# Eight-block transformer on one Trainium2 core: the two routed-expert blocks run on from the attention before them, their routing spread through the loops

## The reference

```
x = x + attention over the 16 heads of each row (width 8), output by Wfc   # stage 5
x = x + experts(layernorm(x))                                              # stage 6
x = x + full attention of batches of 512 rows, 2 heads of 64, with norms   # stage 7
x = x + experts(layernorm(x))                                              # stage 8

experts(x):  logits = x @ Ws.T + bs              # 8 experts
    probs  = softmax(logits); routes = argmax(probs); x = x * max(probs)
    perm   = argsort(routes, stable=True)        # rows sorted by expert
    h = relu(x @ W1[e] + b1[e]);  y = h @ W2[e] + b2[e]
    output: y of each row's expert, in sorted order
```

## Time and profile before

| | us |
|---|---|
| median of 3 runs (lowest, highest) | 1938.3 (1935.96, 1942.25) |
| the profiled execution | 1945.4 |
| its span, first to last instruction | 1943.6 |
| PE, PEld, DVE, ACT, POOL busy | 1622.5, 1160.9, 1223.0, 1069.2, 906.4 |
| granted TensorE clock, mean | 0.911 |

### The profile page before, as it was taken

One profiled execution on the slowest core, in us unless ns is written; L12 is line 12 of the kernel. 1 busy time (PEld: TensorE's weight loads), 2 busy tenths in 40 slices (PEclk: granted clock), 3 DMA queues, 4 the chain that ended last, 5 costly groups with the idle time before them and its releaser, 6 DMA issues.

```text
span 1943.6 us, 37984 instructions
## 1 busy us (share of the span) xinstructions
PE 1622.5 (83%) x13323; PEld 1160.9 (60%) x13323; DVE 1223.0 (63%) x3746; ACT 1069.2 (55%) x2751; POOL 906.4 (47%) x668
## 2 busy tenths in 40 slices
PE   5999997799999966889887789999976666958787
PEld 5999995566666633334544466666644544646565
DVE  3556554887777634555763788777736975636555
ACT  3655563788888724556542578888842113324332
POOL 1333333776666511323443777667613673422134
PEclk8999998999999986999876899999987987968979
DMA  5000000111111100000000111111100001210012
GB/s 206 1 1 1 1 2 6 26 33 31 28 26 29 26 3 1 1 1 1 2 1 1 24 27 32 26 33 26 32 7 0 1 1 38 23 27 1 22 23 23
DMA packets 41082, 38.64 MB, mean 20 GB/s; under 512 B 21944, under 2 KB 32192, under 8 KB 40512
## 3 DMA queue, kind: packets, MB, share of 16 engines
q1 hardware_dynamic: 35264, 32.02, 6.3%
q0 software_dynamic: 5632, 4.20, 1.8%
HBM read 13.14 MB, written 4.20 MB: 9 GB/s over the span
## 4 chain that ended last, share of the span: by engine, by line
PE 46%; DVE 15%; issue 12%; POOL 7%; ACT 4%; POOLq 0%; DMA 0%; DVEq 0%; ACTq 0%; SPq 0%; another core or an unknown queue 0%
PE ps L682 4%; PE ps L328 3%; PE ps L483 3%; PE ps L586 3%; PE ps L492 3%; PE ps L900 3%; PE ps L529 3%; PE ps L908 2%; PE ps L495 2%; PE ps L543 2%; PE ps L598 2%; PE ps L695 2%; PE ps L561 2%; PE ps L502 2%; DVE g_ss L1639 2%
## 5 line engine op out<-in xcount | busy, mean ns | idle before, releaser
L977 ACT ACTIVATE arena<-ps 128x512 f32<-128x512 f32 (+4 forms) x670 | 356.6, 588 | 284.2 <-PE ps L328 103.8
L1214 ACT ACTIVATE arena<-ps 128x320 f32<-128x320 f32 (+4 forms) x256 | 132.4, 561 | 137.4 <-PE ps L682 134.5
L1114 ACT ACTIVATE arena<-arena,g_small 128x128 f32<-128x128 f32 x512 | 198.7, 406 | 0.5
L2197 POOL TENSOR_TENSOR arena<-arena,consts 128x512 f32<-128x512 f32 (+1 forms) x64 | 93.2, 1456 | 196.1 <-ACT arena L1214 196.0
L1610 DVE CUSTOM_DVE_ANT_0 arena<-ps,consts,g_ss 128x128 f32<-128x128 f32 x512 | 145.6, 347 | 58.7 <-PE ps L483 58.7
L2218 POOL TENSOR_TENSOR arena<-arena 128x512 f32<-128x512 f32 x64 | 81.8, 1278 | 176.8 <-DVE arena L1618 176.8
L682 PE MATMUL ps<-arena 32*128 32x160 f32 (+4 forms) x1024 | 122.3, 468 | 20.9 <-ACT arena L1214 10.2
L328 PE MATMUL ps<-consts,arena 128*128 128x128 f32 x400 | 80.9, 340 | 68.7 <-POOL arena L2176 19.5
L1617 DVE TENSOR_TENSOR arena<-ps,tabs 128x512 f32<-128x512 f32 x128 | 87.7, 685 | 52.4 <-ACT arena L1083 44.9
L328 PEld LDWEIGHTS ps<-consts,arena 128*128 128x128 f32 x400 | 55.7, 172 | 106.1 <-POOL arena L2176 24.2
L682 PEld LDWEIGHTS ps<-arena 32*128 32x128 f32 x1024 | 61.9, 213 | 88.6 <-ACT arena L1214 54.2
(11 more groups left out here) (256 smaller groups left out, 4200.0 us busy)
## 6 DMA issues: line engine op xcount, KB each, us to landing
arena<-arena SPq DMA_DIRECT2D x112, 128.0 KB, 2.3
weights<-in_w SPq DMA_DIRECT2D x1, 5069.0 KB, 24.2
weights<-in_w SPq DMA_DIRECT2D x1, 2052.0 KB, 12.7
arena<-Y SPq DMA_DIRECT2D x64, 32.0 KB
arena<-Y SPq DMA_DIRECT2D x64, 31.8 KB
consts<-in_c SPq DMA_DIRECT2D x1, 1278.0 KB, 8.7
sorted_rows<-X SPq DMA_DIRECT2D x1, 1024.0 KB, 5.1
X<-sorted_rows SPq DMA_DIRECT2D x4, 256.0 KB, 3.6
```

The costliest lines, as they stand in the source:

```text
L977: copy = lambda o, i: act.activation(o, i, ACT.Copy)
L1114: last = act.activation(g_p[:, n % 2, 4 * hf + i, :], g_sc[:, 4 * hf + i, :], ACT.Exp, scale=-1.0, bias=g_mn[:, h:h + 1], accum_out=g_rs[: ...
L1214: act.activation(b_p[:, U % 2, 2 * gp:2 * gp + 2, at:at + n], ps[:, b:b + 2, 0:n], ACT.Exp, scale=float(HD) ** -0.5).then_inc(s.b_exp, 1)
L2197: pool.tensor_tensor(v, v, m.unsqueeze(1).broadcast_to([P, NG, n]), ALU.mult)\
```

## The change

1. The experts' part of the arena moves behind that of both attentions (`taken[0] = 12800`), with its own `e_stats`, `e_mv` and `e_bias`. Their PSUM banks are chosen per stage.
2. No barrier between attention and experts: each engine goes from its attention loop straight into `experts(k)`. SP writes `X` to memory as soon as its last row is added.
3. Batch 0 is routed inside the attention's last steps. On DVE in stage 5: variance of batch 0 at t = 8, centre at 9, shift at 12 (ahead of values), route at 13, prefix at 15; batch 1's variance and centre at 12 and 13, batch 2's variance after the loop. In stage 7: variances at 5, 9, 13 and after the loop, centres at 6, 10, 14, shift at 13, route at 14, prefix after the loop. PE's four steps stand at t = 10, 11, 13, 14 and at 9, 12, 14, 15.
4. Batches 1, 2, 3 are routed inside the main loop from units 0, 7, 14 on (`turned_at`). `places_of_all` follows unit 19.
5. The tail of head attention (shift(15), values(14), sums(15), values(15), the last rows) is written out after its loop, its last parts inside units 3 to 7.
6. Unit 0 no longer waits for the biases: it writes `e_acc` (mask times product, no addition); POOL adds batch 0's biases, fetched into `e_bias`, once after unit 7.

The core of the diff: banks and units; PE (stage 5 loop, a front step, main loop); ACT main loop; DVE (stage 5 loop, its tail, unit 0, main loop); POOL. Stage 7 and the functions moved out unchanged are left out.

```diff
-        taken[0] = 0
+        taken[0] = 12800
...
+        front_bank, up_banks, down_banks = (4, 7), ((0, 1), (5, 6)), ((2, 3), (0, 1))
+        turned_at = (None, 0, 7, 14)
...
+                    if t == 10:
+                        turn_routed_x(0, 0)
+                    if t == 11:
+                        logits(0, 0)
+                    if t == 13:
+                        turn_scaled_x(0, 0)
+                    if t == 14:
+                        ranks(0, 0)
+                experts(0, turn_sums, rows_out)
...
+            def turn_routed_x(k, c):
+                z = NB * k + c
+                pe.wait_ge(es.e_ln, z + 1)
+                need(pe, es.e_rank_in, z)
+                if c == 0:
+                    pe.wait_ge(s.m_xT if k else s.c_xT, NB)
...
+                    if k == 0 and q == 6:
+                        turn_sums(NB - 1)
+                    if k == 0 and q == 7:
+                        rows_out(NB - 1)
+                    for c in range(1, NB):
+                        if q == turned_at[c]:
+                            turn_routed_x(k, c)
+                        elif q == turned_at[c] + 1:
+                            logits(k, c)
+                        elif q == turned_at[c] + 5:
+                            turn_scaled_x(k, c)
+                        elif q == turned_at[c] + 6:
+                            ranks(k, c)
...
+                    if k == 0 and q == 4:
+                        norm_routed(0, 2)
+                    if k == 0 and q == 6:
+                        keep_sums(NB - 1)
+                    if q == (11 if k == 0 else 4):
+                        norm_routed(k, 3)
+                    for c in range(1, NB):
+                        if q == turned_at[c]:
+                            keep_routed_x(k, c)
+                        elif q == turned_at[c] + 2:
+                            exps_routed(k, c)
+                        elif q == turned_at[c] + 5:
+                            keep_scaled_x(k, c)
...
                     if 0 <= t - 1 < TT:
                         shift(t - 1)
+                    if t == 12:
+                        shift_routed(0, 0)
                     if 0 <= t - 2 < TT:
                         values(t - 2)
                     if 0 <= t - 1 < TT:
                         sums(t - 1)
+                    if t == 13:
+                        route(0, 0)
+                    if t == 15:
...
+                    if t in (7, 11, 15):
+                        add_rows((t - 7) // NT)
+                    if t in (8, 12):
+                        variance(0, t // NT - 2)
+                    if t in (9, 13):
+                        centre(0, t // NT - 2)
+                shift(TT - 1)
+                values(TT - 2)
+                sums(TT - 1)
+                variance(0, 2)
+                experts(0, values, add_rows)
...
+                        if q == 0:
+                            ins = ts(e_acc[:, i, :], ps[:, down_banks[k][0], j * P:(j + 1) * P], e_oh[:, i, 0:1], None,
+                                     ALU.mult)
+                            continue
...
+                    if k == 0 and q == 3:
+                        values(TT - 1)
+                        centre(0, 2)
+                    if k == 0 and q == 7:
+                        add_rows(NB - 1)
+                        variance(0, 3)
+                    if q == (9 if k == 0 else 1):
+                        centre(k, 3)
+                    for c in range(1, NB):
+                        if q == turned_at[c]:
+                            shift_routed(k, c)
+                        elif q == turned_at[c] + 1:
+                            route(k, c)
+                        elif q == turned_at[c] + 5:
+                            prefix(k, c)
+                    if q == turned_at[3] + 5:
+                        places_of_all(k)
...
+                fetch_biases(0)
+                fetch_biases(1)
+                if k == 0:
+                    root_routed(0, 3)
+                fetch_biases(2)
+                pool.wait_ge(b2_sem[0], 16 * NT * (k + 1))
+                pool.wait_ge(es.e_acc_in, (E * NB - 1) * k + E)
+                pool.tensor_tensor(e_acc[:, 0:NT, :], e_acc[:, 0:NT, :], e_bias, ALU.add).then_inc(es.e_bias_in, 1)
+                fetch_biases(3)
```

More of the change, by code:

```diff
@@ new lines, in full_attention, with norm_routed @@
+                    if t in (7, 11, 15):
+                        norm_routed(1, t // NT - 1)
+                    if t == 9:
+                        keep_routed_x(1, 0)
+                    if t == 13:
+                        exps_routed(1, 0)
+                    if t == 14:
+                        keep_scaled_x(1, 0)
+                experts(1)
+            def norm_routed(k, c):
+                act.wait_ge(es.e_nm, NB * k + c + 1)
+                for i in range(NT * c, NT * c + NT):
+                    last = act.activation(e_xl[:, i, :], X[:, i, :], ACT.Identity,
+                                          scale=e_rstd[:, i:i + 1], bias=e_nm[:, i:i + 1])
+                last.then_inc(es.e_ln, 1)
@@ new lines, in full_attention, with by_expert, variance @@
+                    if t in (5, 9, 13):
+                        variance(1, t // NT - 1)
+                    if t in (6, 10, 14):
+                        centre(1, t // NT - 1)
+                    if t == 14:
+                        route(1, 0)
+                dve.wait_ge(s.m_out, TT)
+                variance(1, 3)
+                prefix(1, 0)
+                experts(1)
+            def by_expert(ap):
+                return ap.unsqueeze(2).broadcast_to([P, NT, E])
+            def variance(k, c):
+                for i in range(NT * c, NT * c + NT):
+                    last = dve.bn_stats(e_stats[:, i, :], X[:, i, :])
+                after(last)
+                for i in range(NT * c, NT * c + NT):
+                    last = dve.bn_aggr(e_mv[:, i, :], e_stats[:, i, :])
+                after(last)
+                ts(e_rstd[:, NT * c:NT * c + NT], e_mv[:, NT * c:NT * c + NT, 1], EPS5, None, ALU.add)\
+                    .then_inc(es.e_var, 1)
@@ new lines, in places_of_all @@
+            def places_of_all(k):
+                dve.wait_ge(es.e_rank_in, NB * k + NB)
+                for e in range(E - 1):
+                    after(tt(e_eo[:, e + 1:e + 2], e_eo[:, e:e + 1], e_pre[:, TT, e:e + 1], ALU.add))
+                after(tt(e_pos, e_pos, wide(e_eo, [P, TT, E], 1), ALU.add))
+                after(tt(e_pos, e_pos, e_oh, ALU.mult))
+                after(dve.tensor_reduce(e_m[:, 5], e_pos, AX, ALU.add))
+                dve.tensor_copy(e_idx[:, :], e_m[:, 5]).then_inc(es.e_idx_in, 1)
```

401 lines of the change are left out of this document (159 added, 242 removed).

## The result

The changed kernel takes 1931.8 us (median of 7 runs, 1928.1 to 1937.8) where the kernel before took 1940.1 beside it: a ratio of 0.9963, 95% interval 0.9948 to 0.9978, or 7.2 us less. In nine later runs it gave 1931.9 and the same 0.9963. The direction was forecast, the size was not: 19.3 us were predicted, and 1919 with 1907 to 1931.

What follows compares the result with a forecast made beforehand. POOL's sends, starting when the places end, were taken to bound both expert stages' ends. Gains of 7.7 us in stage 6 and 11.6 in stage 8 made 19.3, so 1938.3 - 19.3 = 1919 us, range 1907 to 1931.

Steps and rivals of the forecast that it cites:

- Port waits: Head attention: DVE's small operations wait for POOL's mixes, 2.9 us at t = 8, 9, 12, 4.9 at 13; none beside fetches.
- PE's lower clock in head attention: Stage 5, t = 14: PE's sum takes longer after idleness, 1.2 us taken from between 0 and 2.8.
- Unit 0 to the places in stage 6: Stage 6: DVE's own work of 41.4 us plus waits of 10.3, from 1618.6 to places ending at 1670.3.
- The exit: Stages 6 and 8: sixteen POOL sends in a row at 1.86 us end 29.8 us after the places.
- rival of a slow memory: Exits of both stages: sends at 3.1 us each would cost 37 more, giving 1956; chance 0.05.
- Full attention: Stage 7: batch 0's routing adds 7.9 us, 3.8 of it in step 14; then 2.2 for turning, up(1) and down(0).
- The end: After stage 8's last send: no added time was predicted.
- 7.7: Stage 6: us gained, its sends ending at 1700.1 against 1707.8.
- 11.6: Stage 8: us gained, its sends ending at 1928.7 against 1940.3.
- the scale: Whole kernel: the profile's 1945.4 lies 7.1 us above the median, so 19.3 was subtracted from 1938.3.
- gain is eaten: Rival: route's locked operations meet more mixes, or waits double, leaving the time within 0.3%, 1932.5 to 1944; chance 0.13.
- a late e_probs stops PE in stage 7: Stage 7, part of the rival of chance 0.13: a late e_ln or e_probs stops PE for all; no separate size.

Runs made afterwards that it cites:

- e_dve_early: Changed kernel with batch 0's variance, centre and route in head attention put behind the products, ahead of the maxima: ratio 0.9955 to the kernel before.
- e_exps_first: Changed kernel with ACT's exponentials put ahead of its copy of the turned sums at t = 6, 10, 14: 1918.5 us, ratio 0.9887 to the kernel before.
- e_before_exps: The kernel before with its exponentials of steps 6, 10 and 14 put ahead of the copy of the turned sums: ratio 0.9963.
- e_spacing8: Changed kernel with batches 1 to 3 routed eight units apart, not seven, places behind unit 21: ratio 0.9976 to the kernel before.
- e_six_apart: Changed kernel with batches 1 to 3 routed six units apart, places behind unit 17, batch 2 in a second PSUM bank: ratio 0.9928 to the kernel before.
- e_fill: Changed kernel with unread matmuls where PE waits in head attention, full attention's step 14 and stage 8's opening: ratio 0.9946 to the kernel before.
- e_all_five8: Changed kernel with exponentials first, early statistics and route, scores(15) ahead of turning, routing six units apart, in stage 8 five: 1903.1 us, ratio 0.9813.

## Why the prediction was wrong

**Port waits.** Right. Steps 8, 9, 12 and 13 of head attention grew by 2.9, 2.8, 2.9 and 4.6 us; 2.9, 2.9, 2.9 and 4.9 were forecast. Nothing of the kind shows beside POOL's fetches: route beside them takes 0.2 an operation. That the operations aren't long for themselves e_dve_early and the other places show: the centre took 2.92 us beside a mix and 0.15 in stage 7. What a barrier is worth by itself no run shows.

**PE's lower clock in head attention: this step failed.** The prediction gave it 1.2 us, at t = 14 alone, and took the place where it would strike from PE's idleness. Step 14 grew by 1.2 to 1.7, but step 10 by 3.0 in two of the six executions that share this code with the change, by 1.7 in one and by 0.1 in three, and it had been forecast at nothing: 1.9 us more in the mean of the four profiles that give the 231.0. Unit 0 came 146.7 to 150.8 us after the first products; 146.4 was forecast. The trace of before had the coupling on show, 8.0 for step 10 where steps 8 and 9 took 6.1, and I didn't ask why: the exponentials stand behind a copy that stands behind PE's sum. I had treated head attention as a chain of DVE and POOL to which PE is a bystander. e_exps_first shows it: with that order mended step 10 lasts 6.1 and step 14 6.1, with all the port waits still there. Against e_before_exps the change then brings 7.5 us in stages 5 and 6, or 9.6 from products(8) on.

**Unit 0 to the places in stage 6.** 50.6 and 52.3 us, 51.7 forecast; the wait ahead of unit 5 is 2.47, 3.2 forecast, and all the waits together are 9.6 in the first profile, 10.3 forecast. Right. **The exit:** sixteen sends at 1.87 in both stages, the last ended 30.0 and 29.8 behind the places; unit 31 done 4 us before send 12. Right, and e_spacing8 and e_six_apart move the end as the places move. The rival of a slow memory is out.

**Full attention: two terms too small, again by the lower clock.** The statistics, centres and logits cost 0.9, 0.1 and 0.8 a step as forecast. Step 14 costs 5.2, forecast 3.8: turning and scores took 3.2 us in place of 1.7. Unforecast are 1.0 to 1.6 in step 7 or 11: the second profile's step 11 lasts 7.5, before 5.95, and its values took 3.34 us where before's took 2.02, in windows of granted clock 0.79 and 1.00 (first line the changed kernel's second profile, second line the kernel before):

```profile
1806.00:1814.00 8.00, 7.72 (x47) 6.83 (x48) 4.17 (x10) 4.12 (x10) 0.00 (x0) 0.79 0.00 1
```

```profile
1807.00:1815.00 8.00, 5.34 (x43) 4.48 (x42) 4.74 (x9) 2.94 (x7) 1.83 (x1) 1.00 0.00 0
```

From maxima(5) to maxima(15) the stage grew by 9.9 and 10.4 us, where 7.9 was forecast. And unit 0 waits 4.2 and 3.8, forecast 2.2, since up and down ran at the lower clock. These surpluses don't add up to what lacks, because one thing went the other way, and that was luck: values(15) had run at the lower clock in before, and did not in the changed kernel (first line before, second line changed):

```profile
1836.99 3.63 PE L842 MATMUL ps<-arena 128*128 128x128 f32 x16 [0.83 <-ACT arena L977]
```

```profile
1835.51 2.02 PE L862 MATMUL ps<-arena 128*128 128x128 f32 x16 [0.46 <-ACT arena L1002]
```

So unit 0 came 143.9 and 144.3 us after the reload, 2.3 and 2.7 later than the 141.6 forecast; from there to the places it took 45.7 and 46.1, forecast 44.8. Over the four profiles behind the 219.4 the two excesses are 1.6 and 1.6 us, and the remaining 1.1 of the 4.3 that lack is the profile of before that I subtracted from. That the lower clock costs step 14 and the wait of unit 0 some 2.7 us is shown by e_fill; for steps 7 and 11 and the loop it is read from the clock alone.

**The end: a term put at nothing.** 2.2 us come on behind the last send in every kernel that has the change, and none in the kernels without it. It is not the data: the last send's landed 3.3 us after its start in the second profile of either kernel (in the changed one a send took 4.7, but that was the fifth of the sixteen), and SP had seen all of it 1.7 to 1.8 us after the last send's end, with the change and without. What ends later is POOL's DRAIN at the end of the program, 3.1 us behind the last send in before and 5.3 in the changed kernel (its length in ns, three times the same, then its start; the last sends end at 1940.30 and 1920.75; first line before, second line changed):

```profile
L116 POOLq DRAIN  x1: 9631/9631/9631, 1933.7 to 1933.7; - x1
```

```profile
L116 POOLq DRAIN  x1: 16319/16319/16319, 1909.7 to 1909.7; - x1
```

A broken row of sends doesn't bring it back, nor do engines that finished as late as before: in e_all_five8 unit 31 ended 6.6 us ahead of the last send's end, as in before, and the 5.5 stayed. Why POOL's DRAIN takes 2.2 us longer stays open.

**The sum.** 7.7 lost 3.5: 2.1 from products(8) on, nearly all of it step 10, and the rest in steps 0 to 7, which the change doesn't touch. 11.6 lost 4.3: about 1.6 up to unit 0, 1.6 from there to the places, 1.1 by the scale. 2.2 went at the end: 9.3 remain by the profiles, 7.2 by the timed runs, and the 2 between are less than either can tell. The scale was off because I subtracted from a median of three runs a sum that was made on one slow execution, whose stretches were 0.4 and 1.1 us over the mean of its kernel. The rival "gain is eaten" had the nearest region (1932.5 and up, the time is 0.7 below it) and mostly the wrong mechanism: no mix was caught between pieces of route. Its remark that a late e_probs stops PE in stage 7 came nearer: PE waited 3.19 us there.

## What to carry over

A wait that is put into a loop is priced with everything that queues behind it on the other engines, and the places to look at are the steps of the old trace that are already longer than their neighbours. Ask of each queue what stands ahead of the operation on the path for no reason of data: moving one call behind another took 13.4 us off the changed kernel and about 7 off the kernel before, where the whole change brought 7.2. Where PE waited more, its work took 1.6 to 1.9 times as long afterwards, so an overlap that adds waits elsewhere is worth less than the time that it covers; and profile the kernel before more than once before a sum of 20 us, 1% of the time, is made on it. When such a sum has been measured, compare it term by term: here one term came out right with 2 us of luck in it, and two that were wrong partly cancelled.

## What the runs showed of the hardware

- The same sum after the same 2.91 us of idleness took 6.65 us in one execution and 3.72 in another, at granted clocks of 0.66 and 1.00.
- The kernel before took 1932 to 1946 us in 15 executions on one chip, at mean granted clocks of 0.919 and 0.908 for the two ends.
- Two matmuls of 512 columns that nobody reads, put into PE's wait, kept the next groups at the upper clock: 0.66 and 1.13 us in place of 1.11 and 2.08.
- A DVE operation of 4 to 32 elements beside a mix of POOL took 1.1 to 2.9 us with one SBUF input or two; beside POOL's indirect fetches, 0.2. The Trainium skill (SBUF — State Buffer, Who interferes with whom) lets a GpSimd operation that reads SBUF shut out a DVE operation with two SBUF inputs. It also names `tensor_scalar` among the operations that can take the shared pair with one input, in their two-port modes. The trace agrees with both: `SCALAR_TENSOR_TENSOR` 2.92, `TENSOR_TENSOR` 2.55, and `TENSOR_SCALAR` with one SBUF input 1.70, each ended within 0.1 us of the mix.
- The end of the program came 5.5 us behind the last send where it had come 3.3 behind it, though the data had landed as early; POOL's DRAIN there ended 5.3 and 3.1 us behind the send.
